# A graph layer on one core: 108 of 391 edge chunks summed by TensorE instead of 96, under a schedule computed at build time

## The reference, cut to what matters

```
h = relu(layernorm(x))                                     # 6250 x 128
xw = h @ W_in
W_ij = (shifted_softplus(edge_attr @ W_f1 + b_f1) @ W_f2 + b_f2) * edge_weight
x_ij = xw[dst] * W_ij                                       # 200000 x 128
out = segment_sum(x_ij, src, 6250)
return x + shifted_softplus(out @ W_o1 + b_o1) @ W_o2 + b_o2
```

## Time and profile before

| | |
|---|---|
| time, median of 3 runs | 2441.78 us (2440.59 to 2443.26) |
| the profiled execution | 2439.41 us, its span 2437.6 us |
| granted TensorE clock, mean | 0.966 |
| PE busy | 2132.0 us, 87% |
| POOL busy | 1935.9 us, 79% |
| DVE busy | 1790.4 us, 73% |
| ACT busy | 1737.7 us, 71% |
| DMA packets of the scatters (q0) | 35.4% of 16 engines' span |

### The profile page before, as it was taken

One profiled execution on the slowest core, in us unless ns is written; L12 is line 12 of the kernel. 1 busy time (PEld: TensorE's weight loads), 2 busy tenths in 40 slices (PEclk: granted clock), 3 DMA queues, 4 the chain that ended last, 5 costly groups with the idle time before them and its releaser, 6 DMA issues.

```text
span 2437.6 us, 54860 instructions
## 1 busy us (share of the span) xinstructions
PE 2132.0 (87%) x15903; PEld 1381.0 (57%) x16098; DVE 1790.4 (73%) x3773; ACT 1737.7 (71%) x4085; POOL 1935.9 (79%) x1240
## 2 busy tenths in 40 slices
PE   2688999999999998999999999999999999999935
PEld 1555556665556565555556555565565565555613
DVE  8667777777777777777777777777777777777747
ACT  1577777777777777777777777777777777777703
POOL 2388888888888888888888888888888888888863
PEclk9889999999999999999999999999999999999968
DMA  8366666666556665666566666565566566666564
GB/s 350 109 96 90 87 90 91 87 94 90 86 92 90 86 94 87 88 92 87 88 92 90 84 93 90 85 93 90 84 92 90 86 90 91 87 90 92 76 169 172
DMA packets 360143, 244.45 MB, mean 100 GB/s; under 512 B 90419, under 2 KB 347137, under 8 KB 359711
## 3 DMA queue, kind: packets, MB, share of 16 engines
q0 software_dynamic: 170912, 80.62, 35.4%
q1 hardware_dynamic: 187715, 159.83, 24.9%
q10 hardware_dynamic: 1212, 0.42, 0.1%
HBM read 141.43 MB, written 99.27 MB: 99 GB/s over the span
## 4 chain that ended last, share of the span: by engine, by line
DMA 42%; POOL 22%; issue 21%; PE 8%; DVE 4%; ACT 1%; POOLq 0%; ACTq 0%; SPq 0%; DVEq 0%
DMA acc<-region,target 42%; POOL acc L591 21%; PE ps L1276 2%; PE ps L1295 2%; PE ps L1255 1%; PE ps L1245 1%; PE ps L1262 1%; ACT region L713 1%; DMA w_f<-in_L_gnn_W_f_dram 1%; PE ps L1326 0%; POOLq L590 0%; DVE region L1150 0%; DVE mean L853 0%; DVE variance L861 0%; DVE region L1165 0%
## 5 line engine op out<-in xcount | busy, mean ns | idle before, releaser
L591 POOL DMA_INDIRECT acc<-region,target x1180 | 1878.8, 1592 | 376.6 <-issue 267.0
L1276 PE MATMUL ps<-region 128*128 128x386 bf16 x2688 | 580.9, 337 | 71.1 <-ACT region L722 70.4
L722 ACT ACTIVATE region<-ps 128x386 bf16<-128x386 f32 x672 | 331.6, 493 | 231.6 <-PE ps L1276 195.5
L1295 PE MATMUL ps<-region 64*128 64x448 bf16 x4032 | 453.4, 358 | 17.9 <-DVE region L1067 13.4
L745 ACT ACTIVATE region<-ps,cut_col 128x128 f32<-128x128 f32 x1564 | 440.3, 363 | 0.6 <-PE ps L1326 0.6
L1255 PE MATMUL ps<-w_f,region 128*128 128x128 f32 x3128 | 428.8, 282 | 13.1 <-issue 2.4
L1255 PEld LDWEIGHTS ps<-w_f,region 128*128 128x128 f32 x3128 | 427.8, 198 | 12.1
L1276 PEld LDWEIGHTS ps<-region 128*128 128x128 bf16 x2688 | 232.4, 97 | 315.6 <-ACT region L722 109.7
L1002 DVE SCALAR_TENSOR_TENSOR region<-ps,bf_negative,region 128x512 f32<-128x512 f32 x391 | 291.3, 745 | 123.8 <-ACT region L708 84.0
L993 DVE TENSOR_SCALAR moved<-region,weight_limit,spare_row 128x4 f32<-128x4 f32 x295 | 97.3, 330 | 374.3 <-ACT region L713 247.4
L1262 PE MATMUL ps<-region 128*128 128x129 f32 x2360 | 327.4, 279 | 28.9 <-DVE region L1002 24.5
(11 more groups left out here) (128 smaller groups left out, 1690.6 us busy)
## 6 DMA issues: line engine op xcount, KB each, us to landing
dst_b<-dst_rows SPq DMA_DIRECT2D x391, 128.0 KB
src_b<-src_rows SPq DMA_DIRECT2D x295, 128.0 KB
acc<-region,target POOLq DMA_INDIRECT x1180
attrT<-in_edge_attr_dram SPq DMA_DIRECT2D x782, 20.0 KB
acc<-region SPq DMA_DIRECT2D x20, 640.0 KB, 17.4
xwin<-xw_parts SPq DMA_DIRECT2D x391, 31.5 KB
region<-acc SPq DMA_DIRECT2D x48, 256.0 KB, 4.7
xw_parts<-parts SPq DMA_DIRECT2D x12, 384.0 KB, 2.3
```

Of the source, the lines that this page charges most:

```text
L591: nc.gpsimd.indirect_dma_start(out=acc[a], out_offset=bass.IndirectOffsetOnAxis(ap=target[:, slot, t:t + 1], axis=0), in_=summed[:, slot, ...
L722: nc.scalar.activation(binned[:, h, j, :], binned_ps[:, 0:PC], ACT.Copy).then_inc(s_binned, 1)
L1276: ins = MM(binned_ps[:, 0:PC], place[:, h % 2, t, j * P:(j + 1) * P], payload_high[:, h % 2, t, :], start=(t == 0), stop=(t == T - 1))
L1295: ins = MM(ps[6 + r][:, 0:NL], binned[rows, slot, j, part * F:(part + 1) * F], in_node[rows, i, slot, :], start=(d == every[0] and part == ...
```

## The change

- `U`, `ON_PE` and `NPE`: the PE chunks are now those with n % 25 in 2, 6, 9, 13, 16, 20, 24, the first 108 of them, at distances of 3 or 4 steps. 283 chunks are left to POOL. The prologue's bins, ranks and digits are made for 108 chunks.
- The tables of offsets are replaced by a loop at build time. It gives every sort the next free half step (one early, one late in each step), not before the late half of the step three after the chunk; each half of a dense product a step of its own, as soon as its tiles are sorted; node one-hots two steps ahead of the product, the addition one step behind.
- In DVE's step the one-hot and the addition to `accT` come first, then `move` and `aim`, the node one-hots, `duplicates`, places, and the payload last ahead of `combine`. The payload is made over two steps: its middle part in step n+1, its low part in step n+2. Places of tiles 0 and 1 are made in step n, 2 in n+1, 3 in n+2 (before: 0 in n, 1 in n+2, 2 and 3 in n+3).
- `in_node` is addressed by the parity of the tile pair's number; `local_f` lies over `bin_i` to make room.

```diff
-U = 16
-ON_PE = (3, 7, 11, 15)
+U = 25
+ON_PE = (2, 6, 9, 13, 16, 20, 24)
+NPE = 108
...
-        BINNED_AT = {4: (0,), 5: (1, 2), 6: (3, 4), 7: (5, 6)}
         OLD, NEW = (3, 2), (1, 0)
-        NODES_AT = ((4, 0, OLD), (5, 0, NEW), (6, 1, OLD), (7, 1, NEW))
...
+        PLACED_AT = ((0, (0, 1)), (1, (2,)), (2, (3,)))
...
+        for kk in range(NPE + SLOTS - 1):
+            for i in range(JT if kk < NPE else 0):
+                j = tile_of(kk % SLOTS, i)
+                earlier = kk - ((kk - 1 - j // 2) % SLOTS + 1)
+                freed = (summed_in[earlier, j % 2], 1) if kk >= SLOTS else (0, 0)
+                turn = max(next_turn(turn), (pe_chunks[kk] + 3, 1), freed)
+                sorted_in[kk, i] = turn
+                sorts_at.setdefault(turn[0], []).append((kk, kk % SLOTS, i, turn[1]))
+            for i in tiles_summed(kk):
+                for ages in (OLD, NEW):
+                    for d in ages:
+                        if holds(kk, d):
+                            step, late = sorted_in[kk - d, place_of((kk - d) % SLOTS, tile_of(kk % SLOTS, i))]
+                            ready = max(ready, step + 2 + late) if d != ages[0] and holds(kk, ages[0]) else step + 2 + late
+                    if any(holds(kk, d) for d in ages):
+                        last = max(last + 1, ready)
+                        nodes_at.setdefault(last - 2, []).append((kk, kk % SLOTS, i, ages))
+                        sums_at.setdefault(last, []).append((kk, kk % SLOTS, i, ages))
+                summed_in[kk, i] = last
+                adds_at.setdefault(last + 1, []).append((kk, kk % SLOTS, i))
...
+                    n = k - 1
+                    if on_pe(n):
+                        kk = pe_index[n]
+                        after(dve, s_msg, n)
+                        V.tensor_copy(payload[:, kk % 2, :, 3 * F:PC], digits[:, bass.ds(kk, 1), :, :].rearrange("p o t d -> p (o t) d"))
+                        V.tensor_tensor(part_of(kk, 1), part_of(kk, 0), high_of(kk, 0), ALU.subtract).then_inc(s_mid, 1)
+                    n = k - 2
+                    if on_pe(n):
+                        kk = pe_index[n]
+                        wait(dve, s_mid, kk + 1)
+                        V.tensor_tensor(part_of(kk, 2), part_of(kk, 1), high_of(kk, 1), ALU.subtract).then_inc(s_pay, 1)
```

More of the change, by code:

```diff
@@ L294, in known @@
             return type(c) is int
-        pe_index = {c: kk for kk, c in enumerate(c for c in range(NU * U) if c % U in ON_PE)}
+        pe_chunks = [c for c in range(NCH) if c % U in ON_PE][:NPE]
+        pe_index = {c: kk for kk, c in enumerate(pe_chunks)}
+        assert len(pe_chunks) == NPE
         pe_counts = [0] + list(itertools.accumulate(int(c in pe_index) for c in range(NCH)))
@@ L379, in holds, with tiles_summed, next_turn @@
         def holds(kk, d):
             return 0 <= kk - d < NPE
+        def tiles_summed(kk):
+            return range(2 if kk % SLOTS < SLOTS - 1 else 1)
+        sorts_at, nodes_at, sums_at, adds_at = ({} for _ in range(4))
+        sorted_in, summed_in = {}, {}
+        turn, last = (0, 0), 0
+        def next_turn(t):
+            return (t[0], 1) if t[1] == 0 else (t[0] + 1, 0)
+        for kk in range(NPE + SLOTS - 1):
[18 more added lines that the diff above has]
+                adds_at.setdefault(last + 1, []).append((kk, kk % SLOTS, i))
@@ L731, in step @@
                         take_sums(n % 4)
-                    jobs = binnings(k)
-                    for job in jobs[:1]:
-                        take_binned(*job)
+                    jobs = sorts_at.get(k, ())
+                    for kk, h, i, late in jobs:
+                        if not late:
+                            take_binned(kk, h, i)
                     n = k + 1
@@ L747, in step @@
                         last.then_inc(s_xg, 1)
-                    for job in jobs[1:]:
-                        take_binned(*job)
+                    for kk, h, i, late in jobs:
+                        if late:
+                            take_binned(kk, h, i)
                 hybrid_steps(step)
@@ L910, in bins @@
                 for r, k in enumerate(ON_PE):
[L911 to L912 removed]
+                    n = len(range(r, NPE, len(ON_PE)))
+                    last = V.tensor_copy(pe_src[:, r:NPE:len(ON_PE), :], src_int[:, k:k + (n - 1) * U + 1:U, :])
                 link(last)
@@ L1016, in step @@
                 def step(k):
[L1017 to L1023, removed]
                     n = k + 1
@@ L1029, in step @@
                                         ALU.is_equal).then_inc(s_oh, 1)
[L1030 to L1043, removed]
+                    for kk, h, i in adds_at.get(k, ()):
                         j = tile_of(h, i)
@@ L1310, in step @@
                         same_product(n % 2, (T - 1,)).then_inc(s_sp, 1)
-                    jobs = binnings(k)
-                    for job in jobs[:1]:
-                        bin_up(*job)
+                    jobs = sorts_at.get(k, ())
+                    for kk, h, i, late in jobs:
+                        if not late:
+                            bin_up(kk, h, i)
                     n = k + 1
```

80 lines of the change are left out of this document (35 added, 45 removed).

## The result

The changed kernel took 2414.63 us in the median (2413.26 to 2416.13, 4 runs) against 2442.52 us before; the ratio is 0.9884, with an interval of 0.9867 to 0.9902. It is 28 us faster. I had forecast 11 us, with a range of 2408 to 2460: direction and range hold, the size is off by more than half.

The account below looks back on a forecast made before the run. The prediction took POOL's scatters as the bound before and PE's pace after. Its terms, -27 + 7 + 4 + 4 + 3 - 1 = -10 us, gave 2431 us, with a range of 2408 to 2460.

Parts of the forecast that it names:

- POOL is the bound before; PE is after.: In the loop: POOL has no free time before; with 12 chunks moved off it, PE's own pace sets the time.
- PE's floor, -27 us: PE's steps in the loop, counted by kind, sum to 2191 us against 2217.8, with ends of -38 and -19.
- POOL's ring, +7: POOL, 97.5% loaded, still makes PE wait for take_sums through the four buffers: +7 us, from 0 to half of 75.8.
- the lower clock behind its waits, +4: Two or three of PE's waits for take_sums bring the 1.2 GHz clock, 1.6 us each: +4 us.
- The end of the loop, +3: Nine dense halves follow the last same product at the lower clock before x is reloaded: +3 us, from -3 to +5.
- Prologue +4, epilogue -1: Larger groups for more PE chunks cost +4 us ahead of the loop; accumulators loaded early give -1 us after it.
- DVE: 0: In DVE's new step order combine is ready about 0.6 us before PE asks for it: cost 0.
- rival 3: DVE is late with combine in 54 steps, so PE's same product waits 0.79 us: +43, 2474 us; chance 0.10.
- Rival 2: The ring still stops PE before the hidden product: 2472 us if half the waits stay, 2458 if a third; chance 0.22.
- the 2196 that I gave as a sign: Sign of being right: PE's last same product about 2196 us after the loop's first hidden product.
- Rival 4: PE's floor is lower than read and POOL stays the bound: 2359 us, chance 0.03; a half-way case of 2400, 0.04.
- Rival 5: Two sorts in a row bring PE's clock down in 104 steps, 1.6 us each: +166, 2597 us; chance 0.02.

Follow-up runs that it names:

- pool_pad_long: The changed kernel with a 128x512 memset on POOL ahead of each POOL chunk's scatters; 2492.11 us, ratio 1.0209.
- pool_pad: The changed kernel with a 128x256 memset on POOL ahead of each POOL chunk's scatters; 2415.65 us, ratio 0.9891.
- planned_102: The changed kernel with 102 PE chunks (2, 6, 10, 13 of 15) instead of 108; 2418.79 us, ratio 0.9907.
- early_first_108: The changed kernel, its planner allowed to begin a chunk's sorts in the early half of step n+3; 2410.74 us, ratio 0.9857.
- early_105: The changed kernel with 105 PE chunks and a chunk's sorts allowed to begin in the early half of step n+3; 2390.50 us, ratio 0.9775.
- early_105_sooner: The changed kernel with 105 PE chunks, sorts allowed from the early half, and places 0, 4, 7, 11, 15, 18, 22 of 26; 2389.11 us, ratio 0.9788.
- old_dve_order: The changed kernel with DVE's step put back in the order of the kernel before; 2496.37 us, ratio 1.0229.
- add_late: The changed kernel with DVE's addition to accT and the node one-hots moved behind the payload; 2522.43 us, ratio 1.0313.
- planned_96: The changed kernel with 96 PE chunks at the old places (3, 7, 11, 15 of 16); 2441.12 us, ratio 0.9996.

## Why the prediction was right in direction and wrong in size

- *POOL is the bound before; PE is after.* Right: chain, scatters and pool_pad_long show it.
- *PE's floor, -27 us.* Right as a total, 2191 us forecast and 2189.64 measured, with slips that nearly cancel. I took the hidden product at 106.50 for the one of step 0, but it is that of step 1, so one start step of 4.8 us was counted too many. Single-sort steps took 5.53 us, not 5.15 (+6 us); those without a dense product 5.02, not 5.3 (-3 us). Full steps were 5.69 and steps without a same product 5.55, as read.
- ***The step that failed: POOL's ring, +7, and the lower clock behind its waits, +4.*** Both were put on top of the floor because POOL would be 97.5% loaded. Beyond the floor PE waited nothing for it: the 6.0 us for L719 are 13 waits of at most 0.5, those of the single-sort steps, and one step of the loop ran at the lower clock. pool_pad shows that even 100% costs nothing over this loop, and pool_pad_long that there is a cost once POOL's need is well above PE's floor. I treated the ring, a store that takes up such irregularities, as if each of them went through it to PE. Two thirds of the error are here (11 of 16 us).
- *The end of the loop, +3.* It was -0.3. The first dense halves after the last same product still ran at full clock (1.88 us for 18 matmuls); only those from 2312 us on at the lower.
- *Prologue +4, epilogue -1.* Measured +4.4 and -2.1.
- *DVE: 0.* Right for the new order (one wait of 0.5 us, at 172 us). But rival 3 named the wrong wait and a wrong price. I followed `combine` to the same product and never asked which of PE's waits the addition ends. The cost of losing that cover was 82 us, not 43.
- *Rival 2* (0.22) is refuted at this load and appears with a load of 283 x 0.50 us more. Its own sum was off too: a third of the waits gives about 2455, not 2458, and the last same product, by my terms, would have come 2191 + 11 = 2202 us after the first hidden product, not the 2196 that I gave as a sign. *Rival 4* (PE below its floor): no full step was shorter. *Rival 5* (the clock goes down at the two sorts in a row): the 103 steps with a dense but no same product, each with its 0.58 us wait, all took 5.5 to 5.6 us, none at the lower clock. The rule of the Trainium skill that I had set against the trace (TensorE: Matmul & The Clock Gate, "A second HAM failure mode: psum-queue depth-cycling") says that small idle times between groups of matmuls can make the clock go up and down. For the longer wait at the same place the traces agree in part: behind a 1.40 us one the clock fell in 11 of 27 cases in planned_102, in 4 of 10 in early_first_108, in 2 of 18 in early_105, and in none of 18 in early_105_sooner.

## What to carry to other kernels

When two engines are coupled by a ring of buffers, compare the total need of each and take the larger; add nothing for a load near one unless a trace shows the ring running full. Before giving a step more work, list for every instruction of the helping engine who waits for it in the same step, not only the one that waited before: here an addition that nobody had waited for carried 82 us. And once the bound has moved, look for the point where both engines are full: 105 chunks, with the early half used, were worth nearly as much again (24 us) as the step from 96 to 108 (28 us).

## What the runs showed of the hardware that I had not expected

- A memset on POOL of 0.91 us between scatters cost 0.22 us. By the profile's rows it ran beside the tail of the indirect DMA instruction ahead of it: in pool_pad a scatter of 1.60 us starts at 1305.39, the memset at 1306.42. The 1.55 us of a scatter are thus not all time in which POOL can do nothing else.
- From 135 us on, within the loop, TensorE's granted clock fell to 1.2 GHz behind single waits of about 1.4 us or more or behind two shorter ones close together (0.83 and 0.48 us at 777 us in the kernel before), never behind a 0.58 us one alone, though there were over a hundred of these. But the length of a wait does not settle it. The dense product waited 52 times for 1.2 us or more in old_dve_order and as often in add_late, up to 1.7 us in both, and not one of these waits brought the lower clock, while a sort's 1.40 us did in 11 of 27 cases in planned_102. What decides is open.
- A 3 MB load of x issued while scatters were still running stretched one scatter from 1.55 to 7.08 us and its wait from 0.30 to 5.59 us in planned_102, and to 7.21 and 6.34 us in planned_96. In both that scatter starts 12.6 us after SP issues the load. That the load is the cause is read from the timing and from the other runs: where it was issued within 6 us of the last scatter's start or after it, as in the kernel before (2346.66 and 2351.4), no scatter took more than 2.3 us.
